# The first-layer matrix of each expert block: fetched from DRAM by the sync queue instead of copied from a resident buffer by VectorE

## The reference, cut to what matters

```python
x = x + attention(layernorm(x))             # scores * causal mask, no softmax
xm = layernorm(x).reshape(-1, 128)          # 4096 tokens
probs = softmax(xm @ Wg)                    # 8 experts
topk_p, topk_i = top_k(probs, 2)
for e in range(8):                          # W1[e] is 128 x 256, W2[e] is 256 x 128
    h = relu(xs @ W1[e] + b1[e])
    ye = h @ W2[e] + b2[e]
    ...                                     # kept where the token chose e
out = x + (sum over a token's two choices of p * ye)
```

## Time and profile before

| what | value |
|---|---|
| device time, median of 3 runs | 394.06 us (392.38 to 396.35) |
| profiled execution: span from the first to the last instruction | 355.5 us |
| profiled execution: its own device time | not reported; the median less the span is 38.6 us |
| mean granted TensorE clock in the span | 0.865 of full speed |
| busy in the span: PE / PEld / DVE / ACT / POOL | 244.7 / 178.6 / 246.3 / 195.3 / 225.8 us |
| DMA moved | 25.81 MB, mean 73 GB/s |

### The profile page before, as it was taken

One profiled execution on the slowest core, in us unless ns is written; L12 is line 12 of the kernel. 1 busy time (PEld: TensorE's weight loads), 2 busy tenths in 40 slices (PEclk: granted clock), 3 DMA queues, 4 the chain that ended last, 5 costly groups with the idle time before them and its releaser, 6 DMA issues.

```text
span 355.5 us, 7602 instructions
## 1 busy us (share of the span) xinstructions
PE 244.7 (69%) x1377; PEld 178.6 (50%) x1378; DVE 246.3 (69%) x762; ACT 195.3 (55%) x596; POOL 225.8 (64%) x231
## 2 busy tenths in 40 slices
PE   0799999886895995986874300398997989880000
PEld 0356666543663663654543200398886979780000
DVE  5759999999999999999997525043443435340690
ACT  2334556658286484683566930176665767660550
POOL 6487754488287485783845666167777777775361
PEclk9999999999698796998997555599999999997555
DMA  6930000001000000000000113233344333320991
GB/s 180 306 114 2 1 1 3 0 31 33 8 24 30 15 30 15 23 26 12 30 33 31 47 47 107 62 98 102 94 107 105 102 100 93 106 62 18 331 315 59
DMA packets 32983, 25.81 MB, mean 73 GB/s; under 512 B 4523, under 2 KB 30765, under 8 KB 32960
## 3 DMA queue, kind: packets, MB, share of 16 engines
q1 hardware_dynamic: 28608, 17.03, 17.5%
q0 software_dynamic: 4352, 8.53, 7.3%
HBM read 14.32 MB, written 11.75 MB: 73 GB/s over the span
## 4 chain that ended last, share of the span: by engine, by line
PE 49%; issue 15%; DVE 15%; DMA 7%; POOL 4%; ACT 3%; SPq 3%; DVEq 2%; POOLq 1%; ACTq 0%
PE ps L809 11%; PE ps L904 9%; PE ps L913 9%; PE ps L800 4%; DVE o_sb L569 3%; DMA back<-returned 3%; PE ps L821 2%; PE ps L895 2%; PE ps L841 2%; DVE picked L652 2%; PE ps L829 2%; DMA dispatched<-rows,slot 2%; DVE norm L601 2%; PE ps L799 2%; POOL dispatched L398 2%
## 5 line engine op out<-in xcount | busy, mean ns | idle before, releaser
L418 POOL DMA_INDIRECT returned<-y_sb,xt x72 | 71.6, 995 | 31.5 <-issue 17.5
L398 POOL DMA_INDIRECT dispatched<-rows,slot x64 | 63.2, 988 | 28.0 <-issue 11.7
L378 POOL TENSOR_TENSOR outer<-qkv 128x1024 f32<-128x1024 f32 x32 | 62.7, 1959 | 24.7 <-ACT qkv L461 24.3
L809 PE MATMUL ps<-outer,causal 128*128 128x512 f32 x128 | 67.5, 654 | 0.0
L569 DVE TENSOR_REDUCE o_sb<-prod 128x128 f32<-128x1024 f32 x32 | 64.1, 2003 | 0.1
L530 ACT ACTIVATE hT<-ps,b_col 128x128 f32<-128x128 f32 x144 | 45.1, 364 | 22.8 <-PE ps L904 22.0
L774 DVE TENSOR_TENSOR y_sb<-ps,b_bc 128x128 f32<-128x128 f32 x72 | 21.0, 292 | 51.7 <-PE ps L913 50.9
L904 PE MATMUL ps<-xT,w_of 128*128 128x128 f32 x288 | 46.5, 285 | 3.8 <-ACT xT L523 2.0
L913 PE MATMUL ps<-w_sb,hT 128*128 x288 | 47.8, 289 | 0.5 <-ACT hT L530 0.4
L904 PEld LDWEIGHTS ps<-xT,w_of 128*128 128x128 f32 x288 | 39.1, 197 | 6.1 <-ACT hT L530 3.3
L562 DVE TENSOR_TENSOR prod<-ps,qkv 128x1024 f32<-128x1024 f32 x32 | 38.7, 1211 | 2.6 <-PE ps L809 2.6
(11 more groups left out here) (127 smaller groups left out, 467.2 us busy)
## 6 DMA issues: line engine op xcount, KB each, us to landing
xt<-dispatched SPq DMA_DIRECT2D x72, 66.0 KB, 1.8
back<-returned SPq DMA_DIRECT2D x8, 512.0 KB, 7.4
x_sb<-x SPq DMA_DIRECT2D x8, 256.0 KB, 5.2
out<-x_sb SPq DMA_DIRECT2D x8, 256.0 KB, 3.9
returned<-y_sb,xt POOLq DMA_INDIRECT x72, 2.3
w_sb<-w SPq DMA_DIRECT2D x1, 1024.0 KB, 7.0
w_sb<-w SPq DMA_DIRECT2D x2, 512.0 KB, 7.6
dispatched<-rows,slot POOLq DMA_INDIRECT x64, 2.3
```

The source lines that it names most:

```text
L378: pool.tensor_tensor(outer[:, t, :].rearrange("p (h a b) -> p h a b", h=HEADS, a=DH), k, v, ALU.mult).then_inc(outer_done, 1)
L398: pool.indirect_dma_start(out=dispatched[:, :], out_offset=bass.IndirectOffsetOnAxis(ap=slot[:, t * K + k:t * K + k + 1], axis=0), in_=row ...
L418: pool.indirect_dma_start(out=returned[:, :], out_offset=bass.IndirectOffsetOnAxis(ap=xt[:, t, D:D + 1].bitcast(I32), axis=0), in_=y_sb[:, ...
L809: mm = pe.matmul(ps_run[t % 2][:, u, :], causal[:, :], outer[:, t, 512 * u:512 * (u + 1)], start=True, stop=True)
```

## The change

The host now passes w1 with the row index first (128 rows of 8 x 256 numbers), and it stays in DRAM: the resident buffer `w1_sb` and its load at the start are gone. SP fetches each block's 128 x 256 part (128 rows of 1 KB) into the same ring of four, with a register for the column where the expert's matrix starts. DVE loses the copy and the read of that table; SP gains the read. PE waits for the DMA's semaphore instead of DVE's. In the first group the first four matrices stand between the first four loads of rows, and the other eight after the group's last load of rows; in the later groups a matrix load follows each load of rows.

```diff
@@ sync queue, start
-            sp.dma_start(w1_sb[:, :].rearrange("d (e h) -> d e h", e=E), w1.rearrange("e d h -> d e h")).then_inc(w_ffn, 16)
@@ sync queue, expert blocks
+            def load_w1(i, t, at):
+                wait(sp, h_mm, G * i + t + 1 - W)
+                apart(sp)
+                sp.dma_start(w1_of[:, t % W, :], w1[:, bass.ds(at, H)]).then_inc(w1_in[t], 16)
+
             rows_at = read(mybir.EngineType.SP, row_at[0:1, 0:G], PAD_BLOCK)
+            experts_at = read(mybir.EngineType.SP, w1_at[0:1, 0:G], (E - 1) * H)
             for t in range(G):
+                if t < W:
+                    load_w1(0, t, experts_at[t])
                 load_block(0, t, rows_at[t])
+            for t in range(W, G):
+                load_w1(0, t, experts_at[t])
             with sp.Fori(1, BLOCKS // G) as i:
                 rows_at = read(mybir.EngineType.SP, row_at[0:1, bass.ds(G * i, G)], PAD_BLOCK)
+                experts_at = read(mybir.EngineType.SP, w1_at[0:1, bass.ds(G * i, G)], (E - 1) * H)
                 for t in range(G):
                     load_block(i, t, rows_at[t])
+                    load_w1(i, t, experts_at[t])
@@ vector engine, expert blocks
             def experts_of_group(i):
-                at[0] = read(mybir.EngineType.DVE, w1_at[0:1, bass.ds(G * i, G)], (E - 1) * H)
                 at[OUTPUT] = read(mybir.EngineType.DVE, w2_at[0:1, bass.ds(G * i, G)], (E - 1) * D)
-            def w1_out(i, t):
-                wait(dve, h_mm, G * i + t + 1 - W)
-                dve.tensor_copy(w1_of[:, t % W, :], w1_sb[:, bass.ds(at[0][t], H)]).then_inc(w1_done, 1)
-            run_slots(dve, [(0, w1_out), (OUTPUT, y_out)], BLOCKS, G, experts_of_group)
+            run_slots(dve, [(OUTPUT, y_out)], BLOCKS, G, experts_of_group)
@@ tensor engine, hidden product
-                wait(pe, w1_done, n + 1)
+                pe.wait_ge(w1_in[t], 16 * (i + 1))
@@ host
-        "w1": L0_ffn_W1,
+        "w1": np.asarray(L0_ffn_W1).transpose(1, 0, 2).reshape(128, -1),
```

More of the change, by code:

```diff
@@ L59, in preln_linear_attention_moe @@
     B, L, D = x.shape
-    E, _, H = w1.shape
+    H = w2.shape[1]
+    E = w2.shape[0]
     T = L // P
@@ L114, in preln_linear_attention_moe @@
         wg_sb = sb("wg_sb", [P, E])
-        w1_sb = sb("w1_sb", [P, E * H])
         b1_col = sb("b1_col", [P, E * HC])
@@ L233, in preln_linear_attention_moe @@
         xt_in = [sem(f"xt_in{t}") for t in range(G)]
-        TX_done, xT_done, w1_done, h_mm, hT_done, y_mm, y_done = (
-            sem("TX_done"), sem("xT_done"), sem("w1_done"), sem("h_mm"), sem("hT_done"), sem("y_mm"), sem("y_done"))
+        TX_done, xT_done, h_mm, hT_done, y_mm, y_done = (
+            sem("TX_done"), sem("xT_done"), sem("h_mm"), sem("hT_done"), sem("y_mm"), sem("y_done"))
         dest_done = sem("dest_done")
+        w1_in = [sem(f"w1_in{t}") for t in range(G)]
         return_done = [sem(f"return_done{t}") for t in range(G)]
@@ L512, in _ @@
             act.wait_ge(table_done, 3)
-            act.wait_ge(w_ffn, (3 + HC) * 16)
+            act.wait_ge(w_ffn, (2 + HC) * 16)
             at = {}
@@ L756, in _ @@
             dve.wait_ge(table_done, 3)
-            dve.wait_ge(w_ffn, (3 + HC) * 16)
+            dve.wait_ge(w_ffn, (2 + HC) * 16)
             at = {}
             def experts_of_group(i):
-                at[0] = read(mybir.EngineType.DVE, w1_at[0:1, bass.ds(G * i, G)], (E - 1) * H)
                 at[OUTPUT] = read(mybir.EngineType.DVE, w2_at[0:1, bass.ds(G * i, G)], (E - 1) * D)
-            def w1_out(i, t):
-                wait(dve, h_mm, G * i + t + 1 - W)
-                dve.tensor_copy(w1_of[:, t % W, :], w1_sb[:, bass.ds(at[0][t], H)]).then_inc(w1_done, 1)
             def y_out(i, t):
@@ L883, in _ @@
             pe.wait_ge(table_done, 3)
-            pe.wait_ge(w_ffn, (3 + HC) * 16)
+            pe.wait_ge(w_ffn, (2 + HC) * 16)
             at = {}
```

## The result

The changed kernel takes **410.56 us** (406.25 to 411.17, four runs), the kernel before beside it 395.21: ratio 1.0412, 95% interval 1.0308 to 1.0516, some 16 us. The forecast was 411.0, in 403 to 420. Direction, cause and time came out, but both levels of the sum, the stage's pace before and after, were wrong in a way that the total hides, and most of the experiments are about that.

The account below looks back on a forecast made before the run. The prediction took POOL's scatters as the bound before and SP's loads after; SP's release moved from 327.48 to 343.6, +16.1 us on the 394.06 median gave 410.2, and small upward pushes made it 411, range 403 to 420.

Parts of the forecast that it names:

- both levels of the sum: Expert blocks: a group of twelve takes 15.6 us before, paced by POOL, and 18.67 us after, paced by SP.
- POOL's scatter sets the stage: Expert blocks of the kernel before: POOL's scatters pace them at 1.30 us a block.
- SP becomes the bound: Expert blocks after the change: SP's loads outlast POOL's scatters by 3 us a group.
- pair: SP in the loop: one row load, 0.73 us, and one matrix load, 0.66 us, together cost 1.39 us.
- group: SP in the loop: twelve pairs of 1.39 us plus 1.99 us for boundary and second read, 18.67 us.
- The head: First group on SP: first read at 224.58, block 4's matrix out at 236.45, block 12's rows at 245.2.
- The copies: DVE's 72 copies, 0.28 us each: removing them gains nothing, because POOL covers them.
- The first rival: POOL stays the bound in the expert blocks; only the head, some 2.5 us, is paid: 396.5 us, chance 0.08.
- the second: Rival: DVE's copies held POOL's scatters up; removing them gives 20.2 us back, less 2.5: 376.4 us, chance 0.02.
- The start load: Start of the kernel: dropping the one 1 MB load saves 0 us.
- PE's clock: Expert blocks: falls of some 6.7 us, each costing about 0.5; rival that it stays low: 450 us, chance 0.03.
- the last landing: End of the expert blocks: the last scatter lands near 344, where 327.48 stood before.

Follow-up runs that it names:

- the early profile: Kernel before, unchanged: the profile shown ahead of the prediction, span 355.5 us beside a median of 394.06 us.
- the repeat: Kernel before, unchanged, profiled a second time: span 390.3 us, profiled execution 392.1 us; measured 394.17 us, ratio 0.9998.
- (2): Kernel before, copies kept, plus the changed kernel's 72 matrix loads and 6 table reads on SP into a buffer nothing reads: 404.85 us, ratio 1.0275.
- (3): Changed kernel with the matrix loads and second table read left out in groups 1 to 5: 395.23 us, ratio 1.0035 to the kernel before.
- (4, 5): Six extra SP markers a load in groups 1 to 5: in the kernel before 399.27 us, ratio 1.0104; in the changed kernel 427.21 us, ratio 1.0864.
- (6): Changed kernel with each matrix load cut to a quarter of its columns, as many DMAs: 408.36 us, ratio 1.0375 to the kernel before.
- (9): Changed kernel with POOL's 72 scatters left out, only their semaphore raised: 375.51 us, ratio 0.9517 to the kernel before.
- (8): Changed kernel with the matrix loads, their wait and table read moved from SP to ACT: 413.1 us, ratio 1.0515 to the kernel before.

## Why the prediction was right, and where it was not

**What bounds the kernel.** "POOL's scatter sets the stage" holds for the early profile only. In the repeat POOL waits for results, and the stage runs 21.0 us a group, not 15.6. I had one sign of this and misread it: a span 38.6 us short of the median. It was not time outside the execution (that is 1.8 to 2.0 in every other profile), it was a different execution.

**SP becomes the bound.** Right, and shown: SP's waits for scatters in the loop gone, POOL idle 19.4 us more than in the repeat (15 forecast), the loads alone cost 10 us with nobody reading them (2), all of the loss goes with them (3), and six markers cost 4 us before and 17 after (4, 5). The Trainium skill, "DMA: Bandwidth & Descriptors", section "Issuing engines are not separate DMA queues", holds the initiating time for usually small; a quarter of the bytes in the same number of issues (6) cost the same, so here it is the price.

**Its size.** The terms were those of a stream without stalls, and there they are right: pair 1.39 forecast and 1.38 measured, group 18.67 and 18.85 (heads of groups 2 to 5 in 9, 268.03 to 324.57, by three). The step that failed is the unspoken one, that SP runs through. With stalls a group takes 24.85. The sum survived because the kernel before stalls too: the span of before is 34.8 us longer in the repeat than in the early profile (390.3 less 355.5), that of after 33.0 longer than with plain stores (409.4 less 376.4) and 35.7 longer than without scatters (409.4 less 373.7). Nearly the same amount on both sides leaves the difference: 20.9 or 18.2 us without stalls (376.4 or 373.7 less 355.5), 19.1 between the two profiles with them, 16 in the medians, 16.1 forecast. That the amounts are so near each other was luck; nothing in the prediction said so.

**The head.** Mis-sized by some 3 us, and by 4.5 with the first stalls. The first read began at 225.50 instead of 224.58, but the repeat began at 225.3 too, so this isn't the change. Block 4's matrix went out at 237.84 (236.45 forecast), block 12's rows at 249.70 (245.2). Without scatters (9) it is 248.29, 3.1 us late, and there the parts can be read. The matrix goes out at 237.66, 1.2 late. Landing and product take 3.3 us instead of 2.7 (the landing's median in 9 is 2.4). The next three blocks take 4.55 instead of 3 x 1.07 = 3.21: the sum took PE at full clock, but after standing idle for 1.85 us until this matrix had landed (240.06), PE ran at half clock (0.50 granted from 242 to 244). PE's products in (9), and the window (PE, PEld, DVE, ACT, POOL busy, granted clock, DMA share, GB/s):

```profile
240.15 0.77 PE L907 MATMUL ps<-xT,w_of 128*128 128x128 f32 x4 [1.85 <-issue]
...
241.78 1.06 PE L907 MATMUL ps<-xT,w_of 128*128 128x128 f32 x4
...
244.86 0.61 PE L907 MATMUL ps<-xT,w_of 128*128 128x128 f32 x4
```

```profile
242.00:244.00 2.00, 2.00 (x11) 2.00 (x11) 0.37 (x2) 0.96 (x4) 0.00 (x0) 0.50 0.29 75
```

**The small terms.** The copies were worth nothing (3), but that POOL covers them does not follow: in the repeat it doesn't pace. The first rival (POOL stays the bound) and the second (copies hold POOL up) fell. The start load: no change seen ahead of 225. PE's clock fell and rose and did not stay low, as forecast; what the falls cost behind the first group was not measured.

**Marks that came out otherwise:** the median distance of row loads in the loop was 1.68 and not 1.39, a group 24.85 and not 18.7, the last landing 381.3 and not 344 on the profile's clock. Without scatters (9) the first two are 1.38 and 18.85, so the stalls made the difference; of the 37 us of the last, some 31 are five groups at 6.2.

**Left open:** why the one early execution of before, scatters and all, had no stall; what in an indexed transfer stops SP's sequencer and makes other engines start late; and what paces the repeat, where SP still has 12.9 us of slack and POOL waits for results.

## What to carry to other kernels

Hold the span of a profile against the median of the runs before any term is read from it: here a gap of 38 us meant another execution, not overhead. Cost each small DMA at its issuing step, with markers, waits and register arithmetic, on the queue that everything waits for; here 0.64 us for a matrix of 128 KB and 0.74 for rows of 66 KB (9). And see what runs beside that queue: a sequencer that must run through beside indexed transfers of POOL ran at 0.76 of its pace (18.85 against 24.85 us a group).

## What the runs showed of the hardware that was not expected

- Beside POOL's indexed transfers SP stands still for about 0.70 us at a time, at any kind of instruction: some 55 to 85 times in most runs, 28 in (8), and not at all where they are left out or are plain stores, single long load issues apart. In the repeat and in after, the register instructions of PE, DVE, ACT and POOL have no such record; of ACT, as issuer of the loads (8), the longest is 38 ns:

```profile
L537 ACTq MOVE w_of<-w x72: 29/29/38, 219.0 to 374.5; - x72
```

- A plain store of 64 KB by POOL occupies it for 0.54 us, the indexed one for 0.98:

```profile
301.30 0.54 POOL L430 DMA_DIRECT2D returned<-y_sb  x1 [0.79 <-DVE y_sb L777]
```

- More SP instructions don't mean more stalls in proportion: with six markers a load the kernel before goes from some 55 to 80, the changed kernel from 84 to 58.
